# Three narrow attentions of a fused decoder block in another order: one bank pair for scores, four score lanes, 32x32 tail tiles, biases in the residual

## The reference, cut to what matters

```python
q, k, v = heads(xn @ Wq + bq), heads(ctx @ Wk + bk), heads(ctx @ Wv + bv)   # 16 heads of 8
scores = einsum('bhqd,bhkd->bhqk', q, k) * scale                            # 512 x 154 a head
attn = softmax(scores, axis=-1)
out = einsum('bhqk,bhkd->bhqd', attn, v).reshape(B, 512, 128) @ Wo + bo
x = x + tanh(g) * out
```

## Time and profile before

| | us |
|---|---|
| median of 3 runs | 2459.78 (2454.25 to 2462.27) |
| the profiled execution | 2450.34 |
| its span on the core | 2448.6 |
| PE busy in it | 2070.1 (85%) |
| DVE busy | 1224.5 (50%) |
| ACT busy | 702.1 (29%) |
| POOL busy | 93.2 (4%) |

### The profile page before, as it was taken

The page is one execution under the profiler, slowest core; times in us unless marked ns, Lnnn a source line. Parts: engine busy times, 40 slices in busy tenths (PEclk is TensorE's granted clock), DMA queues, the critical chain, the costliest instruction groups (busy, mean ns, idle before and its releaser), DMA issues. The chain is left out here.

```text
span 2448.6 us, 33104 instructions
## 1 busy us (share of the span) xinstructions
PE 2070.1 (85%) x12226; PEld 1166.4 (48%) x12226; DVE 1224.5 (50%) x2940; ACT 702.1 (29%) x1245; POOL 93.2 (4%) x178
## 2 busy tenths in 40 slices
PE   4689799988898987987799788888888796997997
PEld 3343477763534435554544344444444554543554
DVE  5553222226655655554443364736364575342776
ACT  2332233332233331222132313142422222323221
POOL 0000000000000000000000101010101001000000
PEclk7777899999898998997597688898989876787999
DMA  1320000020000000000000000000000000000000
GB/s 35 111 77 6 1 0 0 0 48 17 0 0 0 0 0 0 0 0 6 14 9 1 0 1 2 1 2 1 1 1 1 1 0 14 14 1 1 1 0 17
DMA packets 36509, 23.68 MB, mean 10 GB/s; under 512 B 14275, under 2 KB 31896, under 8 KB 36405
## 3 DMA queue, kind: packets, MB, share of 16 engines
q1 hardware_dynamic: 34965, 21.93, 3.6%
q10 hardware_dynamic: 1440, 0.29, 0.1%
HBM read 16.04 MB, written 1.05 MB: 7 GB/s over the span
## 5 line engine op out<-in xcount | busy, mean ns | idle before, releaser
L1741 ACT ACTIVATE L2a_qwork<-psum 128x512 f32<-128x512 f32 (+3 forms) x256 | 94.5, 438 | 226.8 <-PE psum L1671 225.4
L452 DVE RECIPROCAL L1x_rsum<-psum 128x512 f32<-128x512 f32 x32 | 107.4, 3356 | 84.1 <-PE psum L343 84.1
L1842 DVE RECIPROCAL L2a_rsum<-psum 128x512 f32<-128x512 f32 x16 | 53.7, 3357 | 153.4 <-PE psum L1686 153.4
L1340 ACT ACTIVATE L0f_hid<-psum,L0f_b 128x512 f32<-128x512 f32 x128 | 87.9, 687 | 142.3 <-PE psum L1292 140.1
L395 ACT ACTIVATE L1x_pT<-psum 77x512 f32<-77x512 f32 x128 | 68.8, 587 | 193.8 <-PE psum L329 193.7
L1305 PEld LDWEIGHTS psum<-expert_arena,L0f_hid 128*128 128x128 f32 x1024 | 118.4, 192 | 12.0 <-issue 11.5
L1292 PE MATMUL psum<-L0f_xnT,expert_arena 128*128 128x512 f32 x256 | 122.7, 625 | 0.0
L1667 PE MATMUL psum<-L2a_qT,L2a_kT 64*128 64x128 f32 (+3 forms) x512 | 108.2, 506 | 15.2 <-ACT L2a_qwork L1741 10.7
L1305 PE MATMUL psum<-expert_arena,L0f_hid 128*128 128x128 f32 x1024 | 119.3, 275 | 0.0
L1455 DVE SCALAR_TENSOR_TENSOR L0f_acc<-psum,L0f_comb,L0f_acc 128x128 f32<-128x128 f32 x128 | 36.0, 344 | 159.4 <-PE psum L1305 159.4
L1824 DVE TENSOR_REDUCE L2a_negmax<-psum 128x2 f32<-128x256 f32 (+3 forms) x128 | 100.8, 821 | 24.3 <-PE psum L1639 24.3
(11 more groups left out here) (553 smaller groups left out, 3948.0 us busy)
## 6 DMA issues: line engine op xcount, KB each, us to landing
expert_arena<-in_L_ffn_w SPq DMA_DIRECT2D x16, 256.0 KB
L1f_gu<-in_L_ffn_gate_up_w SPq DMA_DIRECT2D x8, 256.0 KB, 4.1
resid<-in_x SPq DMA_DIRECT2D x4, 256.0 KB, 6.1
L0x_q<-L0x_qc SPq DMA_DIRECT2D x16, 64.0 KB
L1f_dn<-in_L_ffn_down_w SPq DMA_DIRECT2D x8, 128.0 KB, 4.2
expert_arena<-in_L_ffn_w_gate_up SPq DMA_DIRECT2D x2, 512.0 KB, 5.4
L2x_q<-L2x_qc SPq DMA_DIRECT2D x16, 64.0 KB
L3x_q<-L3x_qc SPq DMA_DIRECT2D x16, 64.0 KB
```

Source lines behind the costliest of these rows:

```text
L452: v.step(nc.vector.reciprocal(rsum[:, g % 2, :], psum[:, 2 * (g % 2) + 1, :]))
L1340: nc.scalar.activation(hid[0:rows, n % RING, :], psum[0:rows, n % 4, :], ACT.Relu, bias=bias).then_inc(s["hid"], 1)
L1741: nc.scalar.activation(pT[:, c % 2, j, PLACE[k]:PLACE[k] + WIDTH[k]], psum[:, 4 + n % 4, k * P:SEQ], ACT.Exp, scale=scale).then_inc(s["pt" ...
```

## The change

All of it is in `narrow_attention` and in the loads for it.

- Units use banks 0,1 alone. Unit n waits for the reduction of unit n-1. Contexts go to bank 0 (`FRONT`), rows and queries to bank 1, and so does the output (`OUT`), which then needs all reductions done, and before the next batch's first unit the addition (`added`).
- Lanes have four banks, 2 to 5, one for each head j of a group; a slot is one group of heads, its four lanes one behind another, each waiting for the exponential of the same lane in the slot before.
- The tail slot computes 16 tiles of 32x32 (`psum[32 * x:..., 2 + j]`) straight from `k4`; `kbd` goes.
- The maxima come in two halves a batch (two groups of heads each): two sets of transposes, two copies, two DMAs.
- Ahead of the loop only the first eight units of batch 0 run, the other eight come in the first slot; and `turned` and the rotation for batch b+1 are in batch b's first slot.
- v's bias is multiplied by `Wo` once, added to the output's bias, multiplied by the gate, and POOL adds it to the residual rows after the layer norm has read them. The bias matmuls go. `Wo` and v's bias are loaded with their rows in another order.

```diff
-    MAIN, LANES, QUADS = 128, 20, 5
-    UNITS = 16
+    MAIN, SLOTS = 128, 5
+    PAIR, WIDE = 8, 136
+    FRONT, SUMS, OUT = 0, 7, 1
...
+                if not rope:
+                    pool.wait_ge(s["bias"], 2)
+                    for b in range(B):
+                        pool.wait_ge(s["xn"], b + 1)
+                        rows = core.resid[:, b * QT:(b + 1) * QT, :]
+                        nc.gpsimd.tensor_tensor(rows, rows, gbo[:].unsqueeze(1).to_broadcast([P, QT, D]), ALU.add).then_inc(s["biased"], 1)
...
-                def scores(f, n0, n1):
+                def scores(n0, n1):
...
+                            if f >= 2:
+                                pe.wait_ge(s["added"], f - 1)
...
-                        if n >= 2:
-                            pe.wait_ge(s["mx"], UNITS * f + n - 1)
+                        if n:
+                            pe.wait_ge(s["mx"], n)
                         for t in (2 * u, 2 * u + 1):
                             for j in (2 * h, 2 * h + 1):
                                 rows = slice(32 * j, 32 * j + 32)
-                                last = nc.tensor.matmul(psum[:, j, (t % 2) * CTX:(t % 2 + 1) * CTX], q4[rows, f % QB, c, t * P:(t + 1) * P],
+                                last = nc.tensor.matmul(psum[:, j % 2, (t % 2) * CTX:(t % 2 + 1) * CTX], q4[rows, f % QB, c, t * P:(t + 1) * P],
...
+                    if c < NG:
+                        for j in range(NG):
                             rows = slice(32 * j, 32 * j + 32)
+                            if n:
+                                pe.wait_ge(s["pt"], NG * (n - 1) + j + 1)
+                            nc.tensor.matmul(psum[:, 2 + j, :], k4[rows, b, c, 0:MAIN], q4[rows, b % QB, c, :], start=True, stop=True).then_inc(s["s2"], 1)
+                        return
+                    for x in range(NG):
+                        for j in range(NG):
+                            rows = slice(32 * j, 32 * j + 32)
+                            if x == 0:
+                                pe.wait_ge(s["pt"], NG * (n - 1) + j + 1)
+                            last = nc.tensor.matmul(psum[32 * x:32 * x + 32, 2 + j, :], k4[rows, b, x, MAIN:KP], q4[rows, b % QB, x, :], start=True, stop=True)
...
                 def output(b):
+                    pe.wait_ge(s["mx"], 16 * min(b + 2, B))
...
-                        last = nc.tensor.matmul(psum[:, 7, t * P:(t + 1) * P], oT[:, t * P:(t + 1) * P], w["wo"][:], start=True, stop=rope)
-                        if not rope:
-                            last = nc.tensor.matmul(psum[:, 7, t * P:(t + 1) * P], core.ones[0:1, :], w["bo"][:], start=False, stop=True)
+                        last = nc.tensor.matmul(psum[:, OUT, t * P:(t + 1) * P], oT[:, t * P:(t + 1) * P], w["wo"][:], start=True, stop=True)
...
-                todo = (0, 0, 2, 4, 7, 10, 13, 16, 16, 16, 16)
...
+                    scoresT(b, 0)
+                    if b:
+                        max_rows(2 * b + 1)
+                        products(b - 1, NG)
+                        sums(b - 1, NG)
+                    else:
+                        scores(8, 16)
+                    if f < B:
+                        turned(f)
+                    if b == 0:
+                        max_rows(1)
+                    scoresT(b, 1)
+                    if b:
+                        output(b - 1)
...
+                    if b == 0:
+                        maxima(8, 16)
+                    else:
                         normalised(b - 1)
-                    if g < B:
-                        contexts(g)
+                    if f < B:
+                        squares(f)
+                        rotated(f)
                     if b:
                         added(b - 1)
                     if f < B:
-                        maxima(f, 0, UNITS // 2)
-                        if g < B:
-                            squares(g)
-                        maxima(f, UNITS // 2, UNITS)
-                    if g < B:
-                        rotated(g)
+                        maxima(n, n + 8)
```

494 lines of the change are left out of this document (256 added, 238 removed).

## The result

The changed kernel takes 2547.86 us in the median of four runs (2545.42 to 2548.60), the kernel before beside it 2457.02 (2449.64 to 2462.27). The ratio is 1.037, with a 95% interval of 1.034 to 1.040: 3.7% slower. The profiled execution has a span of 2543.4 us against 2448.6, 94.8 more. The mean granted clock is 0.84 (0.857 before). PE is busy for 2038.5 us where it was 2070.1, so the change did take work from PE, and lost more than that in waits.

The account below looks back on a forecast made before the run. PE's work and waits were taken to set the time; at unchanged slow shares L0x +60, L2x +27, L3x +28 gave +115 us, 2565 on the profiled run, 2574 as median. Forecast 2500 to 2650 at 0.66; range leaving out two in ten 2485 to 2650.

Parts of the forecast that it names:

- Rival (4): Waits partly covered: half of 17 us in L0x's middle batches, and the wait at the output; 2545, inside the 0.66 forecast.
- The prices of a unit: Score units on one bank pair: each waiting for the previous reduction costs 2.30 us slow, 1.69 fast.
- Batch 2: Loop of each narrow attention: counted as a middle batch like batch 1, in L2x 44.2 us fast, 64.5 slow.
- The wait of 0.8 for the row of maxima: Middle batch, before units 8 to 11: PE waits 0.8 us because ACT has four exponentials in front of the row.
- The start: Ahead of the loop: eight units at 2.30 take the 18.4 us of sixteen at 1.15; L2x and L3x lanes start as before.
- L0x's wait: L0x, after a batch's last sums: reciprocal, products, squares, rotation, transposes, queries' DMAs, together 22.9 us in place of 6.0.
- the slow shares: Share of time at the slow clock, taken unchanged: 0.46, 0.40, 0.36 in L0x, L2x, L3x; sum +115 us.
- The biases: L2x and L3x: six bias pairs a batch saved at over half of 0.72 us each; POOL's addition costed at nothing.
- The last batch: Last batch, without scores: four banks make a slot 3.3 us fast or 5.3 slow; 10 us shorter.
- (1): Fast clock granted throughout: +29 us, so 2489; 2448 if already in the first units; chance 0.18.
- (2): Lanes do not run four wide, or the tiles don't: 62 and 25 us more, so 2661; chance 0.08.
- (3): Clock stays slow in most of the stages: +197 us, so 2657, all slow 2700; chance 0.08 beyond 2650.

Follow-up runs that it names:

- a_lanes2: Changed kernel with a group's four lanes taken from two row groups, so only two run side by side: 2591.90 us, 1.057 of the kernel before.
- b_bias: Kernel before with only the bias matmuls of L2x and L3x removed and their addition done on GpSimd: 2416.93 us, 0.985 of the kernel before.
- a_twopairs: Changed kernel with batch 0's sixteen units alternating between banks 0,1 and 6,7: 2488.60 us, 1.013 of the kernel before.
- b_onepair: Kernel before with all score units on banks 0 and 1, each waiting for the previous reduction: 2685.06 us, 1.095 of the kernel before.

## Why the prediction was right, and where its terms were off

The time came out at 2547.86, 26 us under the 2574 forecast, inside the range. The places of the loss were the ones named. That the number came so close is in part luck: errors of 8 us and more took one another away, as the sums below show. Rival (4) of the prediction has 2545, nearer still, but by waits that are covered, and none was. The sizes come out so, term by term.

**The prices of a unit** held to 0.03 us: 2.30 slow and 1.70 fast for a direct pair, 1.72 with products behind it (1.69 by the sum). A lane group was 1.07 fast, from 1422.05 to 1423.12, where 0.96 was taken.

**The batches of L2x** (fast / slow as predicted; measured, with the clocks of the windows above):

| stretch | predicted | measured |
|---|---|---|
| first lanes to batch 1's units | 25.3 | 25.3 |
| rest of batch 0 | 34.8 / 51.8 | 38.9 at 0.82 |
| batch 1 | 44.2 / 64.5 | 52.9 at 0.77 |
| batch 2 | 44.2 / 64.5 | 49.3 at 0.77 |
| last batch and end | 29.2 / 41.7 | 30.7 at 0.91 |

With a slow share of 0.46 (twice what 0.77 lacks to 1) the forecast for batch 1 is 44.2 + 0.46 x 20.3 = 53.5, and 52.9 was measured. **Batch 2 was a slip in the working, and the largest error in the sums**: it has no contexts, rows and queries, since no batch is left for them, and I took it as a middle batch like batch 1; in L2x, at the same clock, it is 3.7 us shorter. At its own clock the forecast for it was 4 us too long in L2x, 6 in L3x and 7 in L0x, while batch 1 of L3x came out at 55.4 us where the same sum gives 55.6:

```profile
2213.04:2268.48 55.44, 43.29 (x303) 20.99 (x305) 21.23 (x37) 12.41 (x24) 1.26 (x1) 0.72 0.04 8
2268.48:2317.98 49.50, 38.86 (x290) 18.09 (x291) 19.34 (x30) 11.24 (x22) 0.00 (x0) 0.73 0.01 2
```

Within batch 1 two more terms were off. The wait of 0.8 for the row of maxima doesn't exist: the first of units 8 to 11 starts at 1287.59, right where the sums end, since ACT has copied by then. And the tail slot cost 1.07 fast, 1.94 slow, where I took 1.5 and 1.9. By the Trainium skill, "TensorE: Matmul & The Clock Gate" (Part 3, Measured speedup), it would by estimate have been 1.3, and the lane group 1.12; the trace has 1.07 for both.

**The start** was earlier than "about where they did": the first lanes come 2.2 (L2x) and 2.9 us (L3x) sooner after the stage's first layer norm. In L0x they came at 63.4 (65.0 predicted), and batch 1's units at 102.25 (103.6).

**L0x's wait** of 22.9 us was 22.9, though the terms given for it add to 22.7. A middle batch there was 68.0 and 66.0 us against 61.1 / 81.3, at clocks of 0.75 and 0.70, which by the slow shares would be 71 and 73:

```profile
142.73:210.77 68.04, 42.15 (x316) 21.68 (x319) 30.79 (x69) 16.27 (x30) 0.00 (x0) 0.75 0.19 58
210.77:276.80 66.03, 41.90 (x296) 19.81 (x297) 28.85 (x62) 15.19 (x28) 0.00 (x0) 0.70 0.07 14
```

Some 2 us of that are a flaw of the method. I multiplied the slow share of a stretch by all of the difference between the slow and the fast sum, but the long wait, whose price is the same in both, was at 0.67 (146.70 to 169.56), so it took more than its share of the slow time. The rest is batch 2's slip and the two terms above.

**The clock.** That the slow shares stay as before was wrong. Over a whole loop 0.72, 0.77, 0.73 are slow shares of 0.56, 0.46, 0.54 in place of 0.46, 0.40, 0.36. But the stretch up to batch 1's first unit was computed slow already, so the share to put in is that of the rest:

```profile
102.25:308.96 206.71, 140.34 (x1052) 66.50 (x1052) 85.79 (x172) 49.98 (x94) 0.00 (x0) 0.76 0.19 56
1268.52:1440.30 171.78, 133.18 (x1032) 60.55 (x1032) 67.94 (x112) 43.78 (x86) 2.53 (x2) 0.80 0.03 6
2172.32:2350.13 177.81, 139.22 (x1028) 63.33 (x1022) 66.68 (x108) 44.32 (x86) 2.53 (x2) 0.76 0.03 6
```

Those shares are 0.48, 0.40 and 0.48. With them the prediction's own sums give +61, +27 and +36, and +46.4, +18.6 and +27.5 were measured: the sums were 15, 9 and 8 us too long, and batch 2 is 17 of these 32. In L3x the forecast of +28 met the measured 27.5 because a sum 8 us too long stood on a slow share 0.12 too low. That is luck.

| | predicted | measured |
|---|---|---|
| L0x, end of the stage | +60 | +46.4 |
| L2x, loop | +27 | +18.6 |
| L3x, loop | +28 | +27.5 |
| L2x and L3x, ahead of the loop | 0 | -5.1 |
| other stages | 0 | +7.4 |

**The savings.** Four-wide lanes were right (`a_lanes2`). The biases were undersized: 2.2 us a batch at the fast clock; `b_bias` gives 3.3 in L2x at a clock of 0.80, and 4.4 in L3x, with some of the clock in it. They lay on the path almost whole. POOL's addition cost nothing, as said.

**The last batch** was to be "10 us shorter". It is 13 in L0x and L3x (32.2 us in place of 45.3 and 45.1) and 20 in L2x, where from its first lanes to the last addition it takes 30.7 us at a clock of 0.91, and before it took

```profile
1320.63:1371.50 50.87, 42.52 (x156) 15.52 (x152) 11.47 (x18) 11.19 (x20) 0.00 (x0) 0.69 0.00 0
```

50.9 us at 0.69. PE is not busy for 8.3 us in both, since the output of batch 2 now waits for 3.0 where the half slots did (four times 0.7); all of the difference is busy time. Part of it is work removed, and part is that a stretch slow before was mostly fast after; why it was is not shown.

**Rivals.** (1) fell: the clock stood at 0.50 through the first sixteen units of each stage, also at two pairs (`a_twopairs`). (2) fell by `a_lanes2`, which also puts its price at 44 to 48 us in place of 62. (3) is in part true as a mechanism: with the single pair the clock did fall, and cost some 84 us in the order of before, where ten direct pairs a batch stand among dense work. In the changed order the loops stood at 0.72 to 0.77. (4): nothing of L0x's wait was covered. The page "TensorEngine Tiling (Array Packing)" (Key Properties) of the Trainium skill speaks of a drain when the tiling mode changes; the rows agree with 0.1 us for such a change: products take 0.99 between units (1279.08 to 1280.07) and 0.88 before sums (1420.19 to 1421.07). Where a unit follows it costs next to nothing, for a direct pair is no closer: 1.70 against 1.72 with the products between.

**Open:** the 5.9 us between L0x and L2x. The last 150 us of that stretch were at 0.99 before and at 0.92 after, for the same instructions. In the two profiles of the kernel before the stretch took 879.7 and 879.9 us; in every edited kernel it took 885 to 889, also in `b_onepair` (887.3), which has nothing edited in its loads, and in `b_bias`, where L0x's attention is the same. So these 6 us are not a price of this change in particular. What sets them, no run here tells.

## What to carry to other kernels

Before banks are taken from a producer to widen a consumer, count how often the producer's groups stand directly behind one another: each such place costs the whole round trip (here 0.9 us of wait), and one foreign group of that length between two of them hides it. Where a wait can't be removed, ask what else is queued that could stand in it, down to the start of the loop, where banks of later steps are still free. Take a many-part change apart before it is judged: here the plainest of its parts, the biases, was worth 1.5 to 1.9% by itself and was buried under three losses.
